# The six norms of a two-layer gated cross-attention kernel: square root and reciprocal, or one power on GpSimd

## What is computed

```
x = x + tanh(g_xattn[0]) * attention16(layernorm(x), ctx, L0 weights)
x = x + tanh(g_ffn[0])   * moe_top1_of_8(layernorm(x), L0 weights)
x = x + tanh(g_xattn[1]) * latent_attention16(layernorm(x), ctx, L1 weights)
x = x + tanh(g_ffn[1])   * block(layernorm(x))

layernorm(x) = (x - mean(x)) / sqrt(var(x) + 1e-5)
rmsnorm(x,w) = w * x * rsqrt(mean(x*x) + 1e-5)
block(h)     = r + moe_top8_of_32(rmsnorm(r, ln2_w)),  r = h + attention32(rmsnorm(h, ln1_w))
```

## Time and profile before

| | us |
|---|---|
| median of three runs | 1738.02 |
| lowest, highest | 1728.39, 1741.69 |
| the profiled execution | 1731.37 |
| its span, first to last instruction | 1729.6 |

### The profile page before, as it was taken

How to read it: one execution, slowest core, us unless ns; L and a number is a source line. 1 busy time by engine, 2 the same in 40 slices (tenths; PEclk the granted TensorE clock), 3 DMA queues, 4 the chain that set the end, 5 groups by cost and what they waited for, 6 DMA issues and landing times. The chain is left out here.

```text
span 1729.6 us, 19632 instructions
## 1 busy us (share of the span) xinstructions
PE 1516.6 (88%) x6852; PEld 1060.0 (61%) x6852; DVE 913.5 (53%) x1402; ACT 592.5 (34%) x945; POOL 719.9 (42%) x509
## 2 busy tenths in 40 slices
PE   5897798899978999999999977789797978599998
PEld 3675465444446667666667643465555555499997
DVE  3744111356675766767767435745647272444454
ACT  2322121123323433433433433434434332234343
POOL 2731002046646786787876630423323131133231
PEclk8988898599997999999999998989899989699999
DMA  7004112610001101101100020000000000334441
GB/s 277 1 1 154 32 40 67 190 37 22 1 35 52 53 1 52 53 1 52 53 1 18 1 74 2 25 1 24 24 24 24 24 0 3 93 115 126 118 124 47
DMA packets 60297, 88.33 MB, mean 51 GB/s; under 512 B 7557, under 2 KB 44613, under 8 KB 60231
## 3 DMA queue, kind: packets, MB, share of 16 engines
q1 hardware_dynamic: 59206, 85.82, 15.7%
q0 software_dynamic: 1024, 1.64, 0.3%
HBM read 81.92 MB, written 5.41 MB: 50 GB/s over the span
## 5 line engine op out<-in xcount | busy, mean ns | idle before, releaser
L661 POOL TENSOR_TENSOR xc<-xc,prob 121x800 f32<-121x800 f32 x112 | 230.9, 2061 | 70.4 <-ACT prob L891 62.2
L891 ACT ACTIVATE prob<-PS 121x800 f32<-121x800 f32 x192 | 159.3, 838 | 269.2 <-PE PS L1751 266.4
L1219 DVE TENSOR_REDUCE mx<-PS 128x1 f32<-128x482 f32 (+1 forms) x312 | 185.5, 644 | 76.5 <-PE PS L1731 75.7
L585 POOL TENSOR_TENSOR e_wl<-e_wf,e_wh 128x768 fp32r<-128x768 f32 x33 | 70.9, 2148 | 200.8 <-ACT e_wh L815 159.3
L683 POOL TENSOR_TENSOR q<-q,qt 128x400 f32<-128x400 f32 x64 | 66.0, 1031 | 211.5 <-DVE qt L1338 211.5
L1766 PE MATMUL PS<-prob,kvn 121*64 121x400 f32 (+1 forms) x768 | 141.3, 518 | 0.9 <-ACT prob L891 0.9
L1748 PE MATMUL PS<-qs,kth 128*121 128x400 f32 (+1 forms) x384 | 117.4, 389 | 21.0 <-DMA qm<-nml 18.3
L1730 PE MATMUL PS<-kth,qs 128*128 128x482 f32 (+1 forms) x312 | 126.1, 404 | 7.6 <-DVE kl L1212 5.8
L1731 PE MATMUL PS<-kl,qm 66*128 66x482 f32 (+1 forms) x312 | 121.8, 390 | 0.0
L547 POOL TENSOR_TENSOR p<-d,sm 100x800 f32<-100x800 f32 x48 | 73.1, 1522 | 114.3 <-DVE sm L1041 114.3
L1751 PE MATMUL PS<-qm,kl 66*121 66x400 f32 (+1 forms) x384 | 109.6, 369 | 0.0
(11 more groups left out here) (248 smaller groups left out, 3178.0 us busy)
## 6 DMA issues: line engine op xcount, KB each, us to landing
e_wb<-routing SPq DMA_DIRECT2D x32, 400.0 KB, 3.9
wgu<-in_L_ffn_gate_up_proj SPq DMA_DIRECT2D x8, 1024.0 KB, 14.3
krt<-in_ctx_T SPq DMA_DIRECT2D x8, 722.0 KB, 4.2
ksw<-in_ctx_Tswap SPq DMA_DIRECT2D x8, 722.0 KB, 5.9
wdn<-in_L_ffn_down_proj SPq DMA_DIRECT2D x8, 512.0 KB, 8.6
wq<-in_L_ffn_Wq SPq DMA_DIRECT2D x4, 1024.0 KB, 5.2
wo<-in_L_ffn_Wo SPq DMA_DIRECT2D x4, 1024.0 KB, 5.4
e_wf<-in_L_ffn_Wg SPq DMA_DIRECT2D x32, 128.0 KB, 2.1
```

The source lines that it names most:

```text
L661: pool.tensor_tensor(accp, accp, prob[:, n % RING], ALU.add).then_inc(xb["ap"], 1)
L891: act.activation(prob[0:k, n % RING], PS[0:k, 2 * (n % 2):2 * (n % 2) + 2, 0:GC], ACT.Exp).then_inc(xb["ex"], 1)
L1219: dve.tensor_reduce(mx3[:, m, g:g + 1], PS[:, 4 + k % 3, 0:SEG[g][1]], AX.X, ALU.max).then_inc(xb["free"], 1)
```

## The change

- ACT no longer takes the square root; it adds `epsc` and copies the half out of PSUM (`Identity`), into the same `rstd`.
- DVE no longer takes the reciprocal; it waits for the inverse root.
- POOL takes the power -0.5 of the half, as a tensor-tensor instruction of 128x400 whose second operand is a 128x1 constant broadcast along the free dimension. It does so in all six norms, half after half, before it ends the stage.
- One more constant (`power`, 128x1, -0.5) is made at the start, and the counts that wait for the constants go up by one.

```diff
@@ sync
-            sp.wait_ge(made, 13)
+            sp.wait_ge(made, 14)
@@ gpsimd
+            pool.memset(power[:], -0.5).then_inc(made, 1)
-            pool.wait_ge(made, 13)
+            pool.wait_ge(made, 14)
...
+            def inverse_roots(t):
+                n = 2 * NORMS.index(t)
+                for h in range(2):
+                    pool.wait_ge(ns["sd"], n + h + 1)
+                    pool.tensor_tensor(sq[:, 0, half(h)], rstd[:, half(h)], power[:].to_broadcast([P, HALF]), ALU.pow).then_inc(ns["rs"], 1)
+            inverse_roots("n0")
             for t in range(ST_N0, ST_ATT0):
                 end_stage(pool, t)
...
-            for t in range(ST_ATT0, ST_MOE0):
-                end_stage(pool, t)
+            end_stage(pool, ST_ATT0)
+            end_stage(pool, ST_OUT0)
+            inverse_roots("n1")
+            end_stage(pool, ST_N1)
...
@@ scalar, norm
-                    act.activation(rstd[:, half(h)], PS[:, 2 + h, 0:HALF], ACT.Sqrt, bias=epsc[:, 0:1]).then_inc(s["sd"], 1)
+                    act.activation(rstd[:, half(h)], PS[:, 2 + h, 0:HALF], ACT.Identity, bias=epsc[:, 0:1]).then_inc(s["sd"], 1)
@@ vector, norm
-                    dve.wait_ge(s["sd"], n + h + 1)
-                    dve.reciprocal(sq[:, 0, half(h)], rstd[:, half(h)]).then_inc(s["rs"], 1)
                     dve.wait_ge(s["rs"], n + h + 1)
@@ tensor
-            pe.wait_ge(made, 20)
+            pe.wait_ge(made, 21)
```

More of the change, by code:

```diff
@@ L82, in flamingo @@
         epsc = sb("epsc", [P, 1])
+        power = sb("power", [P, 1])
         ln_w = sb("ln_w", [P, 2, NC])
@@ L534, in _ @@
                                pattern=[[1, S]], channel_multiplier=-1).then_inc(made, 1)
-            pool.wait_ge(made, 18)
+            pool.wait_ge(made, 19)
             pool.affine_select(out=hmask[:], in_=hmask[:], compare_op=ALU.is_ge, fill=0.0, base=HD0 - 1,
@@ L598, in _ @@
                                         bounds_check=NT * P - 1).then_inc(ms0["back"][b // HB], 16)
-            for t in range(ST_MOE0, ST_XA):
-                end_stage(pool, t)
+            end_stage(pool, ST_MOE0)
+            inverse_roots("n2")
+            end_stage(pool, ST_N2)
             def rotate_turned(b, n):
@@ L674, in _ @@
             end_stage(pool, ST_XB)
-            for t in range(ST_N3, ST_F):
-                end_stage(pool, t)
+            inverse_roots("n3")
+            end_stage(pool, ST_N3)
+            inverse_roots("r0")
+            end_stage(pool, ST_R0)
+            end_stage(pool, ST_KV)
             with pool.Fori(0, G2) as it:
@@ L691, in _ @@
             end_stage(pool, ST_F)
+            inverse_roots("r1")
             end_stage(pool, ST_R1)
```

## The result

| | before | changed |
|---|---|---|
| median of four runs, us | 1737.3 | 2459.26 |
| lowest, highest | 1728.39, 1741.69 | 2454.74, 2466.36 |
| span of the profiled execution | 1729.6 | 2452.9 |

The changed kernel takes 1.417 times as long (95% interval 1.410 to 1.424). The direction was forecast, the size was not: the measured time lies 529 us above the upper end of the range, 1930.

What follows compares the result with a forecast made beforehand. Each norm's root, reciprocal and product path, ended by a barrier, was taken to appear whole in the span. Twelve powers of 7.75 us, 93.0, less 40.5 gained, lose 52.5 us: median 1738 to 1790, range 1706 to 1930.

Steps and rivals of the forecast that it cites:

- The price of the power: POOL's power on each half in the norms: p = 7.75 us, from 0.76 or 1.03 up to 20.6 us.
- the prediction's formula: Whole span, all six norms: 40.5 - 12p us gained, p being one power's time; pays under 3.4 us.
- The stretches: First `Identity` to last product: 1.82 + 2p us per layer norm instead of 7.89, 2.01 + 2p per RMS norm instead of 8.34.
- the cover for DVE's first product: In each norm, DVE's first product (0.99 us) lies beside POOL's second power as long as p is above 1.
- The loads that go: Five table loads of 1.28 us ahead of ACT's square roots go; their uncovered parts sum to 3.6 us.
- Costed at nothing: Extra constant at the start, SP's DMAs in the norms, PE's clock and DVE's product beside the second power: no cost or gain.
- rival 1: POOL's power is an ordinary pass, p 1.03 us: faster, 1704 to 1712 us for the median; chance 0.20.
- Rival 3: POOL's power is far dearer, p from 12 us up; at 20.6 us a loss of 207 us, 1945; chance 0.20.
- Rival 2: Power costs about as much as root and reciprocal, p 1.9 to 4.8 us: no change, 1721 to 1755; chance 0.15.
- Rival 4: Table loads stay because ACT's `Identity` may need an absent table: 3.6 us of gain go; shifts the others, no own chance.
- PE's clock: Behind the norms' pauses: a longer pause can't make PE's start much worse, already at the lower level of 1.2 GHz.
- The table load: Ahead of ACT's square root: 1.28 us from the trace, against the skill page's 2.66 us per switch, half a drain.

Runs made afterwards that it cites:

- the probe: Fourteen powers of different sizes on tiles of their own, added on POOL ahead of `n0` to the kernel before; about 0.35 us and 0.160 us for each column.
- the multiplication run: The changed kernel with a multiplication in place of the power on POOL, same tiles and waits; 1716.25 us, 0.991 of the kernel before.
- the `Identity` run: The kernel before with `Identity` in place of the square root on ACT, the reciprocal left on DVE; 1732.33 us, ratio 1.0009.
- the turned kernel: The changed kernel with variances made with tokens on the partitions, so POOL's power works on 100x4; 1732.91 us, 0.998 of the kernel before.

## Why the prediction was wrong, step by step

**The price of the power: wrong, and the only step that matters.** The prediction said that no row shows a power, bounded it by 0.76 or 1.03 us and 20.6 us and took 7.75. It is 64.1. The lower bound was the row of a plain POOL multiplication, the upper end twenty of them, a number of steps that was assumed and that no row gave; the value between them was a ratio borrowed from DVE's reciprocal. None of these rows is of a power, and the probe shows that it costs as much as 62 plain multiplications. Why POOL needs so long for it, the runs don't show. The forecast of 52.5 us and the range to 1930 hang on this term. With p = 64.1 the prediction's formula gives 12 x 64.1 - 40.5 = 728.7 us; the span became 723.3 us longer.

**The stretches: right.** 1.82 + 2 x 64.1 = 130.0 us for a layer norm and 130.2 for an RMS norm were worked out; 129.90 to 129.98 and 130.12 to 130.13 are in the trace, so the `Identity` at the root's price, both hand-overs and the product behind the second power held. So did the cover for DVE's first product: it took 1.64 us instead of 0.99 beside the power, and nothing waited for it. For a p near 1 the formula is too low, as the prediction said: in the multiplication run it gives 3.52 us for a layer norm at p = 0.85, and 4.29 to 4.36 are in the trace.

**The loads that go: nearly right.** 3.6 us uncovered were worked out, about 4.0 were found in the trace of the `Identity` run. The parts worked out were 0.39, 0.83, 1.28, 0.83 and 0.29; `n2` was worth 1.6, of which 0.2 lie ahead of the load, where the second half's mean came sooner. The prediction left five further loads uncounted, one that it named and four that it didn't see. The stages outside the norms were 4.4 us shorter in all, and the loads may be the reason; in the `Identity` run, with the same loads gone, they were 1.6 us shorter, and in the multiplication run 0.1. How much these five are worth is left open.

**Costed at nothing: wrong for the DMAs, without effect on the result.** The prediction said that more time for SP's loads gains nothing, which holds, but not that less time costs. SP was done 1.9 us ahead of the last product in `n0` and 1.5 us in `n1` (145.23 against 146.71); once these norms get shorter by more, SP's issuing ends last in them. For the changed kernel this never came into play; for rival 1 it did.

**The rivals.** Rival 1, the ordinary pass, had 1704 to 1712 us; the run with an ordinary pass gave 1716, of which 4 us are SP's. Its guess that PE's clock could stay up came true in one place of one run: with SP's loads moved the granted clock was 1.00 behind `n0`, but 0.50 behind `n1`, where the 32 matmuls took 5.50 us as in the earlier trace rows. The rule of the Trainium skill that was named beside it (page "GPSIMD Engine Reference", section "Elementwise — side-by-side cycle accounting"), 2.6 cycles for each element of an ordinary two-input instruction, doesn't cover the power: at the page's 1.2 GHz it makes 0.87 us for 400 elements, an estimate from the page, and the trace has 0.85 us for the multiplication and 64.1 for the power. Rival 3, far dearer, was the right one, with 0.20, and its end of 20.6 us was three times too low. Rival 2 fell. Rival 4 fell: the changed kernel has six loads left, the same as in the `Identity` run, and none of them at the line of `Identity`.

**PE's clock.** In the pause of `n0`, the window from 13.6 to 141.9, the granted clock is 0.52, about the lower of its two levels, 1.2 GHz. The 16 matmuls behind it take 7.89 us at a mean of 0.71, where the earlier trace rows had 7.30 at 0.77. That a longer pause hardly makes the start worse held: 0.6 us, and not even that can be put down to the pause's length, as the multiplication run had 8.00 us behind a pause of 5.34.

**The table load.** The Trainium skill, page "ScalarE: Activation LUTs", section "What ACT_TABLE_LOAD costs", gives 2.66 us with a drain for each switch. In the runs here the load takes 1.283 us, starts 0.02 us behind the instruction ahead of it (134.79 + 1.11 to 135.92), and the next one starts 0.02 us behind the load (135.92 + 1.28 to 137.22, above). The same page, section "Table sets: the hidden batching unit", says that one set holds both exponential and logarithm, so that a logarithm and then an exponential need one load; in this case each change between them brought one.

## What to carry to other kernels

An operation that no row of the trace shows can't be bounded by rows of other operations: measure it first, alone, in a few sizes, since a probe of a few instructions would have given 0.16 us a column before anything was moved. When the dear unit is a column and the tile holds the same row 128 times, turn the layout before choosing the engine; it was worth 726 us here for the power and 0.6% to 0.8% for the root. When two medians differ by less than 1%, compare the granted clock of their executions before explaining the difference. And when a stage that ends in a barrier gets shorter, look at the queue that issues DMAs in it, for that may end last next.

## What the runs showed of the hardware that was not expected

- GpSimd's power on fp32 costs about 0.35 us and 0.160 us for each column (8 to 400 columns, 4 in the turned kernel), the same for 1, 16, 64 and 128 partitions and for all bases and exponents tried.
- VectorE's product of 128x800, which takes 0.99 us alone, took 1.64 us beside the running power in `n0` (L1024, above) and 1.65 in `n3`. Beside the multiplication in `n0` it was the other way round: the product kept its 0.99 us and GpSimd's multiplication took 1.25 instead of 0.85 us. On these runs the two don't work side by side for free; what they share, the runs don't show.
- The time of PE's 16 matmuls behind `n0` goes with the granted clock and not with the length of the pause ahead of them: 5.64 us at 1.00 (pause of 3.07 us), 7.30 at 0.77 (7.04 us), 7.89 at 0.71 (128.6 us), 8.00 at 0.70 (5.34 us) and 8.67 at 0.65 (6.00 us, in the kernel with a logarithm and an exponential for each half).
